# Delta rule: state and corrections as 32-column weights for the two output products, with one transpose a step to turn them back

## The reference, cut to what matters

```python
def step(S, inp):                    # S: 128 x 32, one per head and sequence
    qt, kt, vt, gt, bt = inp
    S = S * jnp.exp(gt)
    delta = (vt - kt @ S) * bt
    S = S + kt[:, None] * delta[None, :]
    return (S, qt @ S)
...
q = short_conv(hidden_states @ Wq, conv_wq)      # 4 taps over time, then silu
k = short_conv(hidden_states @ Wk, conv_wk)
v = short_conv(hidden_states @ Wv, conv_wv)
q = l2norm(q.reshape(B, T, H, -1))
k = l2norm(k.reshape(B, T, H, -1))
...
o = gated_delta_rule(q, k, v, g, beta)
```

## Time and profile before

| | before |
|---|---|
| median of 3 runs | 2334.2 us |
| lowest and highest | 2334.17 us, 2365.44 us |
| the profiled execution | 2323.66 us |
| its span | 2321.6 us |
| mean granted TensorE clock | 0.839 of 2.4 GHz |
| busy: TensorE, weight loads, VectorE, ScalarE, GpSimdE | 1788.7, 1173.1, 1042.9, 643.7, 684.3 us |

### The profile page before, as it was taken

How to read it: one execution, slowest core, us unless ns; L and a number is a source line. 1 busy time by engine, 2 the same in 40 slices (tenths; PEclk the granted TensorE clock), 3 DMA queues, 4 the chain that set the end, 5 groups by cost and what they waited for, 6 DMA issues and landing times. The chain is left out here.

```text
span 2321.6 us, 29641 instructions
## 1 busy us (share of the span) xinstructions
PE 1788.7 (77%) x10523; PEld 1173.1 (51%) x10582; DVE 1042.9 (45%) x2310; ACT 643.7 (28%) x1066; POOL 684.3 (29%) x1099
## 2 busy tenths in 40 slices
PE   5885876876858887653879999999999976577772
PEld 3343343444325554321356766777676676354661
DVE  4426327227123333154646565566657632233622
ACT  2232232322312121322524334334434411111010
POOL 2002002002000000001576667676666761000042
PEclk8797797788778888786989999999999966788596
DMA  1000000000010000225012212222221120320064
GB/s 32 1 2 19 1 12 8 1 19 1 1 53 20 20 27 13 87 91 114 14 33 46 46 24 41 41 34 46 46 46 30 32 36 25 88 86 18 18 155 111
DMA packets 215797, 89.32 MB, mean 38 GB/s; under 512 B 166441, under 2 KB 208658, under 8 KB 215426
## 3 DMA queue, kind: packets, MB, share of 16 engines
q1 hardware_dynamic: 202658, 66.99, 13.1%
q0 software_dynamic: 6960, 18.88, 2.9%
q10 hardware_dynamic: 6064, 1.86, 0.4%
HBM read 53.39 MB, written 34.31 MB: 38 GB/s over the span
## 5 line engine op out<-in xcount | busy, mean ns | idle before, releaser
L1072 PE MATMUL d_prep<-d_hT,d_w 128*128 128x512 f32 x384 | 216.3, 693 | 29.3 <-DMA d_cw<-L_attn_conv_wq 18.1
L1407 DVE SCALAR_TENSOR_TENSOR d_conv<-d_prep,d_cw,d_conv 128x511 f32<-128x511 f32 (+2 forms) x288 | 214.4, 746 | 39.3 <-ACT d_conv L1266 32.4
L1358 POOL TENSOR_TENSOR d_prod<-d_blk 64x30 f32<-64x30 f32 (+4 forms) x360 | 172.6, 479 | 135.5 <-DMA d_blk<-mid_a_blk 108.3
L1362 POOL TENSOR_TENSOR d_blk<-d_blk,d_prod 64x30 f32<-64x30 f32 (+4 forms) x360 | 183.3, 509 | 28.2
L347 POOL TENSOR_TENSOR a_rstd<-a_rstd,a_mhalf 128x4 f32<-128x4 f32 x4 | 4.1, 1028 | 563.8 <-DVE a_rstd L431 563.8
L322 ACT ACTIVATE a_probs<-a_acc 128x896 f32<-128x896 f32 x128 | 117.4, 917 | 160.3 <-PE a_acc L260 119.2
L1266 ACT ACTIVATE d_conv<-d_prep,d_cw 128x512 f32<-128x512 f32 x96 | 65.8, 686 | 248.3 <-PE d_prep L1072 248.2
L407 DVE COPY a_ot<-a_out 128x512 f32<-128x512 f32 x32 | 20.6, 686 | 233.7 <-PE a_out L227 233.7
L1072 PEld LDWEIGHTS d_prep<-d_hT,d_w 128*128 128x128 f32 x384 | 74.1, 214 | 99.5 <-issue 76.3
L1111 PE MATMUL d_prep<-d_kq 128*128 128x256 f32 x384 | 94.4, 389 | 15.2 <-DVE d_qkT L1439 14.4
L392 DVE TENSOR_REDUCE a_top<-a_acc 128x2 f32<-128x256 f32 (+3 forms) x128 | 97.8, 819 | 7.7 <-PE a_acc L196 7.0
(11 more groups left out here) (348 smaller groups left out, 3897.2 us busy)
## 6 DMA issues: line engine op xcount, KB each, us to landing
mid_gate<-p_gate POOLq DMA_DIRECT2D x4, 768.0 KB, 4.0
mid_v<-p_v_tok POOLq DMA_DIRECT2D x3, 1024.0 KB, 6.0
d_v_h<-mid_v SPq DMA_DIRECT2D x12, 256.0 KB, 5.8
d_gate_h<-mid_gate SPq DMA_DIRECT2D x12, 256.0 KB, 5.4
mid_a_blk<-d_AT SPq DMA_DIRECT2D x48, 64.0 KB, 2.0
d_blk<-mid_a_blk SPq DMA_DIRECT2D x12, 256.0 KB, 3.6
mid_u_blk<-d_blk SPq DMA_DIRECT2D x12, 256.0 KB, 2.9
mid_l_blk<-d_blkT SPq DMA_DIRECT2D x12, 256.0 KB, 3.7
```

The costliest lines, as they stand in the source:

```text
L1072: last = nc.tensor.matmul(PB[f % 2][:], w[:, n % 2, i, k, :], hT[:, k, b * T:(b + 1) * T], start=k == 0, stop=k == CK - 1)
L1358: nc.gpsimd.tensor_tensor(pr, blk[:, 0:t, t:t + 1].broadcast_to([lanes, t, m]), blk[:, t:t + 1, t + 1:BLK].broadcast_to([lanes, t, m]), AL ...
L1362: nc.gpsimd.tensor_tensor(blk[:, 0:t, t + 1:BLK], blk[:, 0:t, t + 1:BLK], pr, ALU.subtract).then_inc(subst, 1)
L1407: ins = nc.vector.scalar_tensor_tensor(dst, PB[f % 2][:, 0:T - j], cw[:, n % 2, f % 2, TAPS - 1 - j:TAPS - j], dst, ALU.mult, ALU.add)
```

## The change

The two output products swap their operands. For from_q, S of a sequence becomes the weights (32 columns) and the queries (128 columns) are streamed; the results of the four sequences go to the four quarters of 32 partitions of DB. The same is done with eps and qkT for own, into LB[2]. Each result is then transposed so ScalarE copies it to SBUF (`keep_past` into `fqT`, `keep_out` into `oqT`), TensorE transposes the 128 by 128 tile back in one operation (`turn_past`, `turn_out`), and VectorE reads the transposed tile. `take_out`, the operation that writes o, moves behind R of the next step, and after the last step behind `convolve(7)`. On ScalarE the work ahead is cut into the steps, with the two copies at the head of each step, and the last copy behind silu and squares of unit 7.

```diff
+            def turn_out(n, c):
+                pe.wait_ge(oqT_ready, CH * n + c + 1)
+                nc.tensor.transpose(LB[2][:, 1, :], oqT[:], ident[:]).then_inc(oq_turned, 1)
+
+            def turn_past(n, c):
+                pe.wait_ge(fqT_ready, (CH - 1) * n + c)
+                nc.tensor.transpose(DB[:, P:2 * P], fqT[:], ident[:]).then_inc(fq_turned, 1)
+
             def turn_keys(n):
                 for b in ORDER:
                     if n and b == 2:
+                        turn_out(n - 1, CH - 1)
                         pe.wait_ge(o_ready, CH * n)
...
                         if c == 1:
                             pe.wait_ge(decayed, BATCH * min(n + 2, D_H))
+                        else:
+                            pe.wait_ge(fs_ready, (CH - 1) * n + c - 1)
                         for b in range(BATCH):
-                            last = nc.tensor.matmul(DB[:, b * P:b * P + D_V], kq[:, n % KQ_BUFS, 1, b, c * P:(c + 1) * P], S[:, b, :], start=True, stop=True)
+                            last = nc.tensor.matmul(DB[32 * b:32 * b + 32, 0:P], S[:, b, :], kq[:, n % KQ_BUFS, 1, b, c * P:(c + 1) * P], start=True, stop=True)
                         last.then_inc(from_q, 1)
+                        turn_out(n, c - 1)
                     if ahead:
                         project(n + 2, 2 * c)
+                    if c:
+                        turn_past(n, c)
                     pe.wait_ge(r_ready, CH * n + c + 1)
...
-                        last = nc.tensor.matmul(LB[2][:, b, 0:D_V], qkT[:, n % 2, b * CH + c, :], eps[:, b, :], start=True, stop=True)
+                        last = nc.tensor.matmul(LB[2][32 * b:32 * b + 32, 0, :], eps[:, b, :], qkT[:, n % 2, b * CH + c, :], start=True, stop=True)
...
+            def keep_out(n, c):
+                act.wait_ge(added, (2 * CH - 1) * n + min(2 * c + 2, 2 * CH - 1))
+                if CH * n + c:
+                    act.wait_ge(oq_turned, CH * n + c)
+                nc.scalar.activation(oqT[:], LB[2][:, 0, :], ACT.Copy).then_inc(oqT_ready, 1)
+
+            def keep_past(n, c):
+                act.wait_ge(from_q, (CH - 1) * n + c)
+                if (CH - 1) * n + c > 1:
+                    act.wait_ge(fq_turned, (CH - 1) * n + c - 1)
+                nc.scalar.activation(fqT[:], DB[:, 0:P], ACT.Copy).then_inc(fqT_ready, 1)
+
+            def recur(n):
+                ahead = n + 2 < D_H
+                if ahead:
+                    begin(n + 2)
+                for c in range(CH):
+                    if c:
+                        keep_out(n, c - 1)
+                        keep_past(n, c)
+                    if ahead:
+                        convolve(n + 2, 2 * c)
+                        convolve(n + 2, 2 * c + 1)
+                keep_out(n, CH - 1)
...
+            def take_out(n, c):
+                dve.wait_ge(oq_turned, CH * n + c + 1)
+                src = LB[2][:, 1, :].rearrange("p (b v) -> p b v", b=BATCH)
+                if c:
+                    dve.wait_ge(fs_ready, (CH - 1) * n + c)
+                    nc.vector.tensor_tensor(by_b(o[:], c), src, from_S[:], ALU.add).then_inc(o_ready, 1)
+                else:
+                    nc.vector.tensor_copy(by_b(o[:], c), src).then_inc(o_ready, 1)
...
                         nc.vector.tensor_tensor(R[:], r_src, R[:], ALU.subtract).then_inc(r_ready, 1)
+                        take_out(n, c - 1)
                         dve.wait_ge(o_ready, CH * n + c)
-                        dve.wait_ge(from_q, (CH - 1) * n + c)
-                        nc.vector.tensor_tensor(from_S[:], DB[:].rearrange("p (b t) -> p b t", b=BATCH)[:, :, 0:D_V], decays_of(0, n, c), ALU.mult)\
+                        dve.wait_ge(fq_turned, (CH - 1) * n + c)
+                        nc.vector.tensor_tensor(from_S[:], DB[:, P:2 * P].rearrange("p (b v) -> p b v", b=BATCH), decays_of(0, n, c), ALU.mult)\
                             .then_inc(fs_ready, 1)
                         if ahead:
                             convolve(n + 2, 2 * c - 1)
...
                 if ahead:
                     take_sums(n + 2, 0)
                     convolve(n + 2, 7)
+                take_out(n, CH - 1)
```

More of the change, by code:

```diff
@@ L954, in layer1_delta_rule @@
         eps, from_S = sb("eps", [P, BATCH, D_V]), sb("from_S", [P, BATCH, D_V])
-        o = sb("o", [P, TILES, D_V])
+        o, oqT, fqT = sb("o", [P, TILES, D_V]), sb("oqT", [P, P]), sb("fqT", [P, P])
         mean2 = sb("mean2", [P, TILES])
@@ L974, in layer1_delta_rule @@
             "mean_ready", "rms_ready", "o_done", "stored", "cchain", "nchain", "rchain"))
+        oqT_ready, fqT_ready, oq_turned, fq_turned = sem("oqT_ready"), sem("fqT_ready"), sem("oq_turned"), sem("fq_turned")
         w_in, v_in = [sem(f"w_in{n}") for n in range(2)], [sem(f"v_in{n}") for n in range(3)]
@@ L1232, in _ @@
                 turn(n + 1, n + 2)
+            turn_out(D_H - 1, CH - 1)
         @block.scalar
@@ L1256, in keep_sums, with begin @@
                 nc.scalar.activation(nsum[:], NB_[:], ACT.Copy).then_inc(nsum_ready, 1)
-            def convolve(n):
+            def begin(n):
                 act.wait_ge(w_in[n % 2], 64 * (n // 2) + 64)
@@ L1261, in convolve @@
                     act.wait_ge(o_ready, CH * (n - 2))
-                for f in range(8):
[L1263 to L1272, removed]
@@ L1273, in convolve @@
-                silu(n, 7)
-                square(n, 3)
+            def convolve(n, f):
+                act.wait_ge(proj, 8 * n + f + 1)
+                if f >= 2:
+                    act.wait_ge(silued, 8 * n + f - 1)
+                nc.scalar.activation(conv[:, f % 2, :], PB[f % 2][:], ACT.Copy, scale=cw[:, n % 2, f % 2, TAPS - 1:TAPS]).then_inc(scaled, 1)
+                if f == 6:
+                    keep_sums(n, 0)
+                if f:
+                    silu(n, f - 1)
+                    if f % 2 == 0:
+                        square(n, f // 2 - 1)
+                if f == 7:
+                    silu(n, 7)
+                    square(n, 3)
@@ new lines, in recur, with prepare @@
+            def recur(n):
[10 more added lines that the diff above has]
+                keep_out(n, CH - 1)
+            def prepare(n):
+                begin(n)
+                for f in range(8):
+                    convolve(n, f)
@@ L1315, in turn @@
                         cut(U[:, rows[b], :], LB[b], lo, hi, u3_e)
-            convolve(0)
+            prepare(0)
             turn(-1, 0)
-            convolve(1)
+            prepare(1)
             turn(0, 1)
             for n in range(D_H):
-                if n + 2 < D_H:
-                    convolve(n + 2)
+                recur(n)
                 turn(n + 1, n + 2)
@@ L1492, in recur @@
                             nc.vector.tensor_tensor(S_decayed[:], S[:], decays_of(2, n, c + 1), ALU.mult).then_inc(s_dec, 1)
[L1493 to L1499, removed]
-                        nc.vector.tensor_copy(by_b(o[:], c), LB[2][:, :, 0:D_V]).then_inc(o_ready, 1)
                 if ahead:
```

## The result

| | changed kernel | before |
|---|---|---|
| median of 20 runs each, in turn on one chip | 2360.27 us (2343.46 to 2396.42) | 2337.33 us (2319.89 to 2379.86) |
| ratio to before, 95% interval | 1.0104 [1.0074, 1.0135] | |
| ratio in a second set (8 runs) | 1.0078 [1.0026, 1.0131] | |
| ten heads with work ahead, two profiled executions | 704.7 and 698.1 us | 667.8 and 674.6 us |

The change costs 18 to 24 us, about 1%. The ratios leave out those executions of either kernel that took over 1.5% longer than its fastest one; the medians hold all of them. The forecast was 2387 us, 53 more than before. The sign was right, the size more than twice too large.

A forecast was written before the change was run, and what follows sets the result against it. Bound: VectorE's loop from_S, `convolve(2c - 1)`, second projection, almost equal to TensorE's queue. 5.6 us a head, ten times +56, head 11 -3.5, sum +53 on 2334.2: 2387 us, range 2350 to 2425.

The forecast's parts named there:

- Steps 1 to 3: Steps of a head with work ahead: late from_S and `convolve` delay the second projection; +1.7 us, then +1.15 us twice.
- Turn, +1.6 us a head: Head's end: last copy queued behind squares of unit 7 makes o, keys and both `sum_squares` late; +1.6 us a head.
- The clock, 0: TensorE's clock falls in the ten heads: as many reasons gone as come, so no change taken.
- my ends of -29 and +26: Clock's limits: -29 us if no head falls any more, +26 us if every head falls once long and once short.
- The 1.0 us for a short fall: Cost of one short clock fall, from head 9 against head 6, used for the clock's upper end.
- Head 10, 0: Head without work ahead; TensorE waits 10.69 us for a DMA after it, so nothing changes.
- head 11, -3.5 us: Last head, at the low clock: from_k starts some 1.1 us a step sooner; -3.5 us with its end.
- The case that I held likeliest: Whole kernel slower by more than 2%, above 2380.9 us; chance 0.50.
- rival 4: Late transposes in the heads cost less, `turn` hides its part behind VectorE: 2371 us, within 2%; chance 13%.
- Rival 1: TensorE's queue alone bounds a step and VectorE catches up; falls go too: 2276 us, faster; chance 5%.
- Rival 3: The new gaps in TensorE's work bring the clock down more: 2413 us; chance 20%.

The follow-up runs named there:

- `convolve` first: Changed kernel with `convolve(2c - 1)` moved on VectorE to right behind R, ahead of the output operation and from_S: 0.9747 of the kernel before.
- from_q alone: Kernel before with only from_q swapped, copied and transposed back, own and the placing of o as before: 1.0316 of the kernel before.
- own alone: Changed kernel with from_q back in its old form without transpose, own still swapped: 0.9951 of the kernel before.

## Why the prediction was right or wrong

**Steps 1 to 3: right.** Forecast: a gap of 1.85 us before the second projection, from_S 2.12 us after the first; measured 1.86 and 2.10. Solve to solve at the full clock went from 7.90, 9.33 and 9.52 us to 7.65, 10.56 and 10.56, and the second projection of step 3 begins 2.84 us behind its solve where it began 1.04 behind. Up to there a head needs 3.8 us more (4.0 forecast). Putting `convolve` ahead of from_S takes the gap away. A group saves 0.53 us as from_q (0.89 to 0.36, 2.5 times faster) and at least 0.44 as own (0.45 forecast). The Trainium skill has "Up to 4×" for a dimension of 32 (TensorEngine Tiling, Theoretical Speedup), and lists the swap with column tiling under Performance Considerations; four times isn't reached here. Its warning on the same page that copies out of PSUM may become the bound (PSUM Bottleneck) fits only loosely: the copies last 0.27 us and cost nothing in steps 2 and 3; what costs is where the consumer stands in VectorE's queue.

**Turn, +1.6 us a head: the step that failed.** Measured: 0.0. It was put as "all of `sum_squares`, which are queued behind: two times 1643.77 - 1642.79 = 0.98 us, until 1645.3". The copy came as late as forecast (squares begin 0.81 us sooner, 0.95 forecast), but the two pairs of sums took 1662.23 - 1661.24 = 0.99 us together, not 1.96: they write four different quarters of columns and ran at once. With one 0.98 us less `correlate` is late by 0.57 us, not by 1.6: it begins 1662.23 - 1652.91 = 9.32 us behind the second projection of step 3, where it began 8.75 behind. I had seen pairs only apart and multiplied. This is 10 of the 16 us.

The other 0.57 us is given back on VectorE: the small operation a times beta takes 0.17 us where it took 0.72 (the medians of twelve heads are 0.18 and 0.72), and the first AT is on time. What makes it long stands in GpSimd's rows. Before, GpSimd is at g_upto (128 by 512) when it begins, and it ends at 1647.54, 0.04 us behind the first of GpSimd's two operations (1646.47, 1.03 us each). In the changed kernel GpSimd is still at the power of d_mean (1663.06 to 1666.33), which hangs on the late o, and the operation takes 0.17 us beside it. This holds in every trace here: in all 69 heads in which a g_upto operation ran when it began, it took 0.44 to 0.74 us and ended 0.03 to 0.04 us behind that one's end; in the 61 beside the power of d_mean and the 14 beside nothing it took 0.17 or 0.18 (12 more ran beside other operations of GpSimd). So the late copy pays back a part of its own price. That is an accident of timing, which I had not forecast, and not every head has it: in the first profiled execution of the changed kernel seven of the twelve take 0.45 to 0.64 us.

So the sum of structure is 10 x 3.8 = +38 us where I had +56.

**The clock, 0: close, for a reason half right.** Before lost 667.8 - 639 = 29 and 674.6 - 639 = 36 us to it (639 is ten times head 6, as in the prediction; head 9 ends some 2 us sooner than the others in both kernels, which leaves the difference as it is). With 67.7 us a head at the full clock, the changed kernel lost 698.1 - 677 = 21 and 704.7 - 677 = 28 us. The change thus gains some 8 us here on average, within my ends of -29 and +26. "As many reasons gone as come" holds as a sum; that the long falls become short ones I did not foresee. The 1.0 us for a short fall was read from head 9, whose `turn` is shorter than head 6's; head 8, with one short fall, took 65.06 us from solve to solve against 63.88, so 1.2 us.

**Head 10, 0, and head 11, -3.5 us: right.** 60.2 and 60.5 us before, 60.6 twice after; head 11 -3.8.

**The sum**: 38 - 8 - 4 = +26 us, against +18 and +24 measured. Some us of this lie within what single executions differ by, so that the sum comes out near is in part luck. The case that I held likeliest, slower by more than 2%, did not come about. The term of turn alone, taken as measured, would have made the forecast 2371 us; that is rival 4's time, "with nothing for turn", and it is the case that came about, though for another reason than it gives: `turn` does not hide the late copy, the sums behind it need half the time. Rival 1, in which TensorE's queue alone bounds a step, needs one operation in another place: "`convolve` first" is its world and took 2.5% off, as much as rival 1 has, and with the copy early too it is 3.4%. Rival 3 is the half change: with from_q alone the clock does fall that deep.

## What to carry to other kernels

A faster form of a product that needs a copy and a transpose has its result later than the slow one, and in a queue that runs in order everything behind its consumer is late with it. Before such a swap, look what stands behind the consumer and isn't fed by it, and put that first; here this one move turned +1% into -2.5%. Then cost the halves of a change and their clock together: here the halves alone gave -0.5% and +3.2%, and both together +1%. And where identical groups are seen in the trace only apart, multiply them only if they use the same part of the array.

## What the runs showed of the hardware

- Four products of 32 weight columns and 512 streamed ones, each into another quarter of columns, took 0.99 us where two took 0.98, though they belong to two groups with a semaphore wait between them.
- In the changed kernel a fall of the clock lasts 3.4 us and costs 1.65 us in a step; in the old one most falls last 10.2 us and cost 4.5. Six useless products in each gap brought the granted clock of the ten heads from 0.96 to 0.99 and the time down by 17 to 24 us.
- Long gaps aren't what a fall needs: with the same thirty gaps of 1.86 us the clock fell 15 to 17 times (changed kernel) and 36 times (from_q alone), and 20 times with fifteen waits of 0.4 us in their place (own alone).
- A VectorE operation on 128 by 16 elements took 0.17 us alone and up to 0.74 us when GpSimd's product of 128 by 512 elements was running: in 69 heads of 69 it ended 0.03 to 0.04 us behind the GpSimd operation. GpSimd's power on 128 by 16 elements (3.27 us) did not hold it up in any of 61.
